# Embedding gathers released by the scaling of an earlier quad in place of its transposes

## The reference

```
e = stack([tbl_f[ids[:, f]] for f in range(26)])        # 512 x 26 x 64
x = layer_norm(dense @ Wd.T)                            # 512 x 128
y = layer_norm(e @ Ws.T)                                # 512 x 26 x 128
y = layer_norm(project 26 -> 32 over the features)      # 512 x 128 x 32
T = concat(x, y)                                        # 512 x 33 x 128
Z = T @ T.T, lower triangle (528 numbers)
out = layer_norm(Zflat @ Wl.T), 384 of 512 kept
h = relu(concat(out, dense) @ W1 + b1); h = relu(h @ W2 + b2); result = h @ W3
```

## Time and profile before

| what | value |
|---|---|
| median of 3 runs | 220.99 us (217.71 to 222.0) |
| the profiled execution | 220.12 us |
| its span, first to last instruction | 218.3 us |
| mean granted TensorE clock | 0.906 |
| TensorE, VectorE, ScalarE, GpSimd busy | 165.1, 122.1, 87.5, 108.3 us |
| gathers (L378) | 104, busy 100.3 us |

### The profile page before, as it was taken

One profiled execution on the slowest core, in us unless ns is written; L12 is line 12 of the kernel. 1 busy time (PEld: TensorE's weight loads), 2 busy tenths in 40 slices (PEclk: granted clock), 3 DMA queues, 4 the chain that ended last, 5 costly groups with the idle time before them and its releaser, 6 DMA issues.

```text
span 218.3 us, 3377 instructions
## 1 busy us (share of the span) xinstructions
PE 165.1 (76%) x1221; PEld 113.8 (52%) x1221; DVE 122.1 (56%) x326; ACT 87.5 (40%) x246; POOL 108.3 (50%) x139
## 2 busy tenths in 40 slices
PE   0736866079586659599788868896399999999985
PEld 0624633034454446446456656555187866579574
DVE  1849642251549174867487156770845789776310
ACT  2142121112324035953235278423362787365252
POOL 2778777652657564736566655574515000082000
PEclk9999999559998855969969999998579999999999
DMA  6496111100111100301111112011101100000000
GB/s 200 116 368 225 20 26 24 30 17 11 24 24 28 25 18 18 73 15 24 24 25 22 25 39 48 18 30 18 27 2 27 36 12 3 2 3 0 0 0 3
DMA packets 7810, 8.99 MB, mean 41 GB/s; under 512 B 3281, under 2 KB 5457, under 8 KB 7538
## 3 DMA queue, kind: packets, MB, share of 16 engines
q0 software_dynamic: 3328, 3.41, 8.1%
q1 hardware_dynamic: 4034, 4.39, 6.1%
q10 hardware_dynamic: 432, 0.97, 1.4%
HBM read 7.98 MB, written 0.00 MB: 37 GB/s over the span
## 4 chain that ended last, share of the span: by engine, by line
PE 41%; another core or an unknown queue 17%; ACT 15%; issue 10%; POOL 8%; DVE 6%; DMA 3%; ACTq 0%
POOL emb L378 7%; PE pz L479 6%; PE py L464 6%; PE pc L443 4%; PE pf L494 4%; ACT ysq L765 4%; PE tu L426 4%; PE pf L511 3%; PE pf L586 2%; ACT z L837 2%; PE py L459 2%; DVE y_ms L1098 2%; PE py L494 2%; DMA index_parts<-index_parts_dram 2%
## 5 line engine op out<-in xcount | busy, mean ns | idle before, releaser
L378 POOL DMA_INDIRECT emb<-tables_dram,rows_at x104 | 100.3, 964 | 60.9 <-issue 26.4
L426 PE MATMUL tu<-mbd,embT 128*128 128x128 f32 x104 | 21.3, 337 | 20.9 <-ACT embT L750 18.3
L1098 DVE TENSOR_REDUCE y_ms<-ysq 128x16 f32<-128x512 f32 x32 | 20.4, 680 | 24.3 <-ACT ysq L765 15.6
L443 PE MATMUL pc<-wbd,emb 128*128 128x192 f32 (+4 forms) x128 | 31.6, 354 | 1.4 <-issue 1.2
L443 PEld LDWEIGHTS pc<-wbd,emb 128*128 128x128 f32 x128 | 21.3, 213 | 19.7 <-issue 14.6
L426 PEld LDWEIGHTS tu<-mbd,embT 128*128 128x128 f32 x104 | 17.2, 230 | 27.4 <-ACT embT L750 21.3
L479 PE MATMUL pz<-T 128*64 128x67 f32 x512 | 24.4, 242 | 6.2 <-ACT gram L776 3.0
L479 PEld LDWEIGHTS pz<-T 128*64 128x64 f32 x512 | 19.8, 148 | 13.5 <-issue 10.6
L776 ACT ACTIVATE gram<-pz 128x268 f32<-128x268 f32 x32 | 12.5, 392 | 32.0 <-remote 20.8
L765 ACT ACTIVATE ysq<-py 128x512 f32<-128x512 f32 x32 | 17.4, 596 | 16.8 <-remote 10.9
L464 PE MATMUL py<-cs,wg 64*128 64x512 f32 x64 | 21.0, 741 | 0.0
(11 more groups left out here) (141 smaller groups left out, 224.8 us busy)
## 6 DMA issues: line engine op xcount, KB each, us to landing
emb<-tables_dram,rows_at POOLq DMA_INDIRECT x104
w<-w_dram SPq DMA_DIRECT2D x1, 1280.0 KB
wl<-wl_dram SPq DMA_DIRECT2D x1, 1024.0 KB
z<-gram SPq DMA_DIRECT2D x24, 32.0 KB
denseT<-denseT_dram ACTq DMA_DIRECT2D x1, 512.0 KB
w<-w_dram SPq DMA_DIRECT2D x1, 512.0 KB
comb_w<-comb_w_dram ACTq DMA_DIRECT2D x1, 311.0 KB, 3.4
sel<-sel_dram SPq DMA_DIRECT2D x1, 240.0 KB
```

The source lines that it names most:

```text
L378: pool.indirect_dma_start(emb[:, 2 * pair + half, :], None, t["tables"], bass.IndirectOffsetOnAxis(ap=rows_at[:, 2 * g + half, j:j + 1], a ...
L426: mm = pe.matmul(TU[i % NTU][:, QUAD + P * half:QUAD + P * half + P], embT[:, i % 2, P * half:P * half + P], mbd[:, :], start=True, stop=True)
L443: mm = pe.matmul(PC[m % NPC][:, :, :].rearrange("p b c -> p (b c)")[:, col:col + n], of, wbd[:, :, :].rearrange("p b c -> p (b c)")[:, at: ...
L1098: dve.tensor_reduce(y_ms[:, m % 2, half, :], ysq[:, half, :, :], AX_X, ALU.add).then_inc(y_ms_ready, 1)
```

## The change

The semaphore in the wait ahead of each quad's gathers is another: `scaled`, which VectorE counts after `scale_rows`, in place of `t_done`, which TensorE counts after `transposes`. The value is the same, so quad i's gathers wait until quad i - 3 is scaled.

```diff
@@ -373,7 +373,7 @@
                 for pair in pairs:
                     g, j = divmod(pair, PAIRS)
                     if pair % 2 == 0:
-                        wait_if_any(pool, t_done, pair // 2 + 1 - QUADS_AHEAD)
+                        wait_if_any(pool, scaled, pair // 2 + 1 - QUADS_AHEAD)
                     for half in range(2):
                         pool.indirect_dma_start(
                             emb[:, 2 * pair + half, :], None, t["tables"],
```

## The result

The changed kernel takes 228.84 us (median of 5 runs, 228.52 to 229.59) against 220.07 us of the kernel before in 5 runs: a ratio of 1.043, 95% interval 1.0385 to 1.0473. It is 8.8 us slower. The forecast was 223.1 us, no change.

A forecast was written before the change was run, and what follows sets the result against it. Waits between engines, no engine being full, were taken to set the time. The profiled 220.12 us plus 3.0 us of late gathers, with late signals at 0, gave 223.1 us; 8-in-10 range 212 to 234.

The forecast's parts named there:

- no change: Whole kernel: time stays within 2%, 216.6 to 225.4 us; chance 0.41.
- part 5, the late signals: TensorE's signals arriving late while gathers fly: up to 4.7 us gained or the hold moves elsewhere; taken as 0.
- the first stall: Late signal for quad 4's transposes, read at 44.7: may come at 39.6 to 40.2, up to 4.7 us gained.
- the same hold: Delay of TensorE's signals while gathers fly: could just wait elsewhere, cancelling the up to 4.7 us gain.
- Its own signs: Forecast wrong if TensorE waits over 6 us for gathers, or waits without releaser change by more than 10 us.
- Late data, the sum's only term: TensorE's transposes of quads 3, 11, 19 and 21 wait for later gathers: 3.0 us, 5.1 without cover, lower end 0.
- The lockstep rival: From quad 7 on, release falls behind the last landing, period 7.6 us instead of 6.52: 228 to 239 us; chance 0.35.
- Its point "against": Against lockstep: gaps between gathers give TensorE free time, and two quads could be released together; no size given.
- the lateness could also be matmuls that ran longer than drawn: TensorE's late signals: gathers would have nothing to do with them, and moving gathers would cost late data alone.
- Slower: Whole kernel beyond the 2% band, by lockstep from quad 7 on: 228 to 239 us, most likely 230; chance 0.35.
- The unexplained share, 37 us: Waiting on the chain that ended last, 17%, which the profile can pin on no instruction.
- faster: Whole kernel: held signals become fewer, a quarter of 37 us unexplained gives 9 us: 211 to 216 us; chance 0.24.

The follow-up runs named there:

- e9: Kernel before, rows by plain DMAs, gathers with the old wait into a buffer nobody reads: 220.33 us beside 220.27 of the kernel before, ratio 1.0045.
- e10: Changed kernel, rows by plain DMAs, gathers with the new wait into a buffer nobody reads: 228.46 us beside 220.27 of the kernel before, ratio 1.041.
- e11: No gathers, rows by 26 plain DMAs from SP's queue: 178.48 us beside 220.27 of the kernel before, ratio 0.815.
- e12: Changed kernel without edit, timed again: median 228.34 us of six runs, lowest 223.17, beside 220.27 of the kernel before, ratio 1.022.
- e15: Changed kernel plus a GpSimd memset of about 1.5 us ahead of each quad's wait from quad 6: 218.86 us against 222.06 before, ratio 0.984.
- e2: Kernel before, rows by plain DMAs, gathers with the old wait into a buffer nobody reads: 178.52 us beside 184.0 of the kernel before.
- e3: Changed kernel, rows by plain DMAs, gathers with the new wait into a buffer nobody reads: 178.97 us beside 184.0 of the kernel before.
- e1: No gathers, rows by 26 plain DMAs from SP's queue: 176.98 us beside 184.0 of the kernel before.
- e7: Changed kernel with no wait at all ahead of the gathers: 290.58 us, ratio 1.316 to the kernel before.
- e14: Kernel before with a lead of two quads, waiting for the transposes of quad i-2: 221.20 us beside 222.06 of the kernel before.
- e18: Kernel before (wait for transposes) plus a GpSimd memset ahead of each quad's wait from quad 6: 217.55 us against 221.72 without it.
- e4: Changed kernel with a lead of four quads, waiting for the scaling of quad i-4: 183.86 us beside 184.0 of the kernel before, ratio 0.997.

## Why the prediction was wrong

**The gathers' price was put at zero.** The step that failed is part 5, the late signals: "the same hold could just wait elsewhere. I take 0 for the forecast". The pattern had been seen, and its first consequence was worked out right: quad 6 would start at 41 to 42 if the first stall shrank, by up to 4.7 us; it started at 41.40, and the stall shrank by 4.75. But the same hold was then left where it was for the 19 quads behind. e9 and e10 put its change at 8.1 us, e9 and e11 the whole of it at 42 us, more than the 37 us of the chain that the prediction named. Its own signs said so: the waits without a releaser of ScalarE and VectorE changed by 15.4 us, where over 10 meant a wrong forecast, and TensorE's waits for gathers were 7.1 us in sum, where over 6 did.

**Late data, the sum's only term, was the wrong term.** The 3.0 us were built from quads 3, 11, 19 and 21. In the trace TensorE waits for data in quads 1 (1.47 us), 3 (0.19 and 2.06), 8 (1.27) and 21 (2.10), 4.9 us more than before. Quad 3, for which 0.65 us were added, waits no longer than it did (2.16), quads 11 and 19 don't wait at all, and quads 1 and 8 were not in the sum. e10 has no such wait and a median 0.1 us from that of the changed kernel on its chip (e12), or some 4 us above it by the undisturbed runs: no run shows that the term cost anything.

**The lockstep rival had the size and half of the mechanism.** It gave 228 to 239 us, with held signals as its cause, and the time fell there. Its price was a period of 7.6 us in each quad. Measured is (177.98 - 49.62) / 18 = 7.13 against 6.52, so 0.61 x 18 = 11 us, of which the earlier head gives back part. But the quads are not evenly late. Six times two come with less than 1 us between them, and a wait of 3.1 to 5.8 us follows. What the rival did not see is that a later release can let bursts run together. A likely reason, not shown, is that VectorE's count of quads can go up twice in short order while TensorE has a backlog, where TensorE's own count cannot. Its point "against", that two quads could be released together, was right as a fact and, by e15, on the wrong side.

**The hardware rules.** The Trainium skill ("SBUF — State Buffer", on the two sides of its ports) says that DMA and compute engines do not contend. Taken by the prediction as a ground for +3.0, it is borne out on one chip by e2 and e3 against e1 (178.5 and 179.0 against 177.0 us), but not by e9 against e11 on another, 42 us apart. The measurement decides that gathers can slow TensorE; whether at these ports is not shown. That "the lateness could also be matmuls that ran longer than drawn" (drawn by the prediction from the Trainium skill, "Perfetto Trace Analysis", the section on the TensorE timeline, which calls a matmul's reported end an estimate) was nearer than the prediction made of it: in e7 it is TensorE that finishes late, and the gathers are the reason; the two were no alternatives.

**The chances.** Slower had 0.35, no change 0.41. The unexplained share, 37 us, was four times what the change moved in the end; the two cases that rested on it, faster and slower, deserved more than their 0.59 together, and the forecast rested on the known waits instead.

Open: by what path gathers slow TensorE, and whether other traffic inside the loop would; why one chip of four shows nothing of it; what besides bursts that run together makes the new times worse; why some runs of the changed kernel take 223 us; and whether recording an execution has a part in it, since every time here comes from recorded ones.

## What to carry to other kernels

A throttle is also a schedule: before moving its release to another engine, ask which engine the throttled work disturbs. Here TensorE's own signal (220 us) was the better release than VectorE's (229) and than none (290); that it is better because it stops the gathers while TensorE has a backlog fits e14 and e18, and is not proven. When a share of the chain has no known releaser and is larger than the effect you forecast, a run that removes the suspect without its data (here into a spare buffer) is worth more than the most careful sum of known waits. Compare kernels only with runs of the same chip: 184 and 221 us were the same program.

## What the runs showed of the hardware

- The same kernel took 184.0 us (13 runs, 183.3 to 185.5) on one chip and 220.3, 221.1, 221.7 and 222.1 us in groups on three others; with plain DMAs in place of GpSimd's gathers it took 177.0 and 178.5 us on a chip of either kind.
- On one of the latter chips, with gathers issued 1.25 us apart without end, TensorE got through one instruction in 1.40 us, where twelve matmuls took 0.57 us a moment earlier; a signal was awaited for 49.7 us (e7).
- On the chip of e1 to e4 gathers issued as closely (e2 to e4, each quad 0.3 us behind the one before) left no wait without a releaser.
- With 3.4 MB of rows by plain DMAs from SP's queue, all in the first 30 us or so, there was no wait without a releaser (e11).
- A gap of 1.3 us between bursts of four gathers took away more than half of the waits without a releaser (60.6, and 59.9 on the same chip, to 28.9 us).
